# The deformable "snake" stage: four slope items handed to TensorE unsummed, and the offset convolution on shifted copies in four column tiles

## The reference, cut to what matters

```
off = tanh(group_norm(conv3x3(x, w_off, b_off)))      # the "offset convolution"; 9 of 18 channels are used
upper, lower = cumulative sums of off away from the centre channel 4
y = row + cumsum_k ; x = column + (k - 4)             # k = 0..8, nine sampling points
v_k = image sampled linearly between two rows at (y clipped, x clipped)
out = relu(group_norm(sum_k w_dsc[:, :, k] @ v_k + b_dsc))
x = x + out
```

## Time and profile before

| | us |
|---|---|
| median of 3 runs | 1713.78 (1711.48 to 1716.94) |
| the profiled execution | 1718.72 |
| its span from the first to the last instruction | 1715.8 |
| start of this stage (first instruction of its block) | 1362.06 |
| item 0 of pass 0 starts on DVE | 1402.80 |
| item 19 of pass 7 ends on DVE | 1699.2 |

### The profile page before, as it was taken

How to read it: one execution, slowest core, us unless ns; L and a number is a source line. 1 busy time by engine, 2 the same in 40 slices (tenths; PEclk the granted TensorE clock), 3 DMA queues, 4 the chain that set the end, 5 groups by cost and what they waited for, 6 DMA issues and landing times. The chain is left out here.

```text
span 1715.8 us, 35545 instructions
## 1 busy us (share of the span) xinstructions
PE 1445.7 (84%) x10772; PEld 643.9 (38%) x10772; DVE 1243.6 (72%) x4972; ACT 978.4 (57%) x1653; POOL 1083.2 (63%) x780
## 2 busy tenths in 40 slices
PE   3999999999999999999928999847777558786775
PEld 1333333333333333333306777536555322121211
DVE  4999999999998999999844445442222456767676
ACT  2588888888887888888823434310000024645454
POOL 3689999989998999999951223220000247867786
PEclk9999999999999999999968999979999879888877
DMA  6000000000000000000005555000000100000000
GB/s 146 8 2 9 4 9 4 10 5 2 9 4 10 5 2 11 2 2 2 2 17 111 111 111 110 0 19 0 0 0 0 44 0 1 1 1 13 1 13 25
DMA packets 16179, 35.48 MB, mean 21 GB/s; under 512 B 5636, under 2 KB 7272, under 8 KB 15996
## 3 DMA queue, kind: packets, MB, share of 16 engines
q1 hardware_dynamic: 14268, 31.96, 8.3%
q10 hardware_dynamic: 1728, 1.35, 0.3%
HBM read 9.47 MB, written 2.10 MB: 7 GB/s over the span
## 5 line engine op out<-in xcount | busy, mean ns | idle before, releaser
L440 POOL TENSOR_SCALAR l_onehot<-l_ib,c_iota 128x512 bf16<-128x512 f16 x256 | 399.9, 1563 | 60.7 <-ACT l_ib L387 60.7
L549 DVE FIND_INDEX8 l_idx<-l_top,l_scored 128x8 uint32<-128x256 f32 x1024 | 411.9, 416 | 0.0
L250 PE MATMUL ps<-l_ct_slot,l_res 32*128 32x512 f32 x2048 | 410.1, 612 | 0.0
L566 DVE CUSTOM_DVE_ANT_0 l_scored<-ps,l_gain 128x256 f32<-128x256 f32 x1024 | 375.8, 412 | 20.4 <-ACT l_gain L369 19.6
L369 ACT ACTIVATE l_gain<-ps 128x768 f32<-128x768 f32 (+1 forms) x384 | 283.8, 739 | 118.3 <-PE ps L250 117.6
L1603 POOL TENSOR_TENSOR l_isum<-l_term 128x512 f32<-128x512 f32 x160 | 204.9, 1309 | 89.1 <-DVE l_term L1701 50.3
L273 PE MATMUL ps<-l_onehot,l_cbp_slot 128*32 128x512 bf16 x3072 | 217.1, 390 | 7.0 <-POOL l_onehot L440 3.3
L244 PE MATMUL ps<-l_csq,l_row_slot 32*128 32x512 bf16 x1024 | 155.1, 396 | 20.3 <-DVE l_top L566 7.3
L250 PEld LDWEIGHTS ps<-l_ct_slot,l_res 32*128 32x128 f32 x2048 | 155.6, 194 | 11.5 <-issue 0.9
L1528 ACT ACTIVATE ps<-ps,l_minus 128x512 f32<-128x512 f32 x192 | 118.2, 662 | 72.6 <-DVE l_term L1707 56.4
L735 PE MATMUL ps<-l_wc,l_xi 100*128 100x192 f32 x768 | 133.4, 331 | 30.7 <-DMA l_xi<-l_xt 30.7
(11 more groups left out here) (158 smaller groups left out, 2048.9 us busy)
## 6 DMA issues: line engine op xcount, KB each, us to landing
l_xi<-l_xt SPq DMA_DIRECT2D x48, 384.0 KB, 7.1
X<-in_x SPq DMA_DIRECT2D x16, 128.0 KB, 7.9
out<-X SPq DMA_DIRECT2D x16, 128.0 KB, 2.2
l_ct<-in_codes_t SPq DMA_DIRECT2D x4, 448.0 KB, 13.5
l_ct_slot<-l_ct SPq DMA_DIRECT2D x7, 256.0 KB, 2.3
l_cbp_slot<-l_cbp SPq DMA_DIRECT2D x8, 96.0 KB, 1.9
l_wt<-in_l_w SPq DMA_DIRECT2D x1, 768.0 KB, 4.3
l_w_off<-in_l_w_off SPq DMA_DIRECT2D x1, 576.0 KB, 3.3
```

Of the source, the lines that this page charges most:

```text
L250: pe.matmul(ps[:, at + n - FIRST[k], :], res[rows, i, P * tt:P * (tt + 1)], ct_slot[rows, par, :], start=False, stop=True, skip_group_chec ...
L440: nc.gpsimd.tensor_scalar(onehot[:, i % 2, g, 0, :], ib16[:, i % 2, g, :], iota[:, 0:1], None, ALU.is_equal).then_inc(s_near, 1)
L549: nc.vector.max_index(idx8[:, i % 2, n, :], top[:, i % 2, n:n + 1].to_broadcast([P, 8]), scored[:, WIDE * (k % 3) + n - FIRST[k], :]).then ...
L566: nc.vector.tensor_tensor_reduce(out=scored[:, WIDE * (k % 3) + m, :], in0=ps[:, WIDE * (k % 2) + m, :PAIRED], in1=gain[:, WIDE * (k % 2) ...
```

## The change

- `DIRECT = 4`: the eight terms of items 0 to 3 go into a ring of four new buffers `slope_term` (`SLOPES = 4`) and PE takes them itself. The new `slope_terms(p, d)` is one group of four for one item (its two terms in the place of two items). POOL adds only items 4 to 19; `terms(p, i)` has 8 turns instead of 10. The wait on `s_partial` moves to `slope_terms(p, 0)`. DVE waits for `s_taken` before it writes a slope buffer again, so item 2 waits until PE has taken item 0.
- The offset convolution reads `xi`, in which SP lays three copies of each image shifted by 0, 1 and 2 columns side by side in 96 partitions (12 DMAs of 32 x 1154 fp32 for each set, 48 in all). One row ky of the 3 x 3 kernel is then four multiplications 96 x 32 x 512, one for each group, each in column tile g. `w_off` shrinks from 128 x 1152 to 96 x 96 fp32.
- PE's hand-written order is new: where the running sums, `own_rows`, `join`, the group averages and the pieces of the convolution stand. `copy_raw(1, j-1, 1)` and `moments(1, j-1, 1)` stand two items later. `down` and `bend` have two slots. The image differences on POOL come after item 4's addition, not item 3's.

```
+DIRECT = 4
+PAIRED_ITEMS = NI - DIRECT
+TURNS = PAIRED_ITEMS // 2
...
+            def columns(j):
+
+                sp.wait_ge(s_xz, START + j + 1)
+                if j:
+                    sp.wait_ge(s_conv, START + 2 * j)
+                flat = xz[:, j].rearrange("p y x -> p (y x)")
+                for g in range(G):
+                    for kx in range(3):
+                        sp.dma_start(xi[C * kx:C * kx + C, g, :SHIFTED],
+                                     flat[C * g:C * g + C, kx:kx + SHIFTED]).then_inc(s_xi, 16)
...
-            def offset_conv(j, h, taps):
...
+            def offset_conv(j, h, kys):
+
+                for ky in kys:
+                    if ky == 0 and h == 0:
+                        pe.wait_ge(s_xi, START + (j + 1) * (16 * 3 * G))
+                    for g in range(G):
+                        at = (ky + ROWS * h) * PADW
+                        rows = xi[:, g, at:at + ROWS * PADW].rearrange("p (y x) -> p y x", x=PADW)
+                        mm = pe.matmul(grid(ps[C * g:C * g + C, SIDE, :]), w_off[:, ky, :], rows[:, :, 0:W],
+                                       start=(ky == 0), stop=(ky == 2), skip_group_check=True)
...
+            def slope_terms(p, d):
+
+                pe.wait_ge(s_term, START + p * NT + 2 * d + 2)
+                if d == 0 and p:
+                    pe.wait_ge(s_partial, START + 2 * p)
+                at = 2 * (p * DIRECT + d)
+                operands = [(ITEMS[d][0], lambda rows, b=(at + e) % SLOPES: grid(slope_term[rows, b, :]))
+                            for e in range(2)]
+                accumulate(operands, d == 0, False).then_inc(s_taken, 1)
...
+                for d in range(DIRECT):
+                    slope_terms(p, d)
+                    if d == 0:
+                        running_sum(p, CUMS + 1)
...
+                for i in range(TURNS):
+                    for c in {0: (4, 5), 2: (6,), 3: (7,)}.get(i, ()):
+                        running_sum(p, c)
...
                     terms(p, i)
...
-                        if i == 1 and j:
-                            pe.wait_ge(s_raw[1], START + 2 * j - 1)
-                            join(p - 1)
-                        if i < 3:
-                            own_rows(p, i)
...
+                        if i == 0:
+                            if j:
+                                pe.wait_ge(s_raw[1], START + 2 * j - 1)
+                                join(p - 1)
+                            own_rows(p, 0)
+                        if i == 1:
+                            own_rows(p, 1)
+                            own_rows(p, 2)
...
-                for n in range(NI):
+                for n in range(DIRECT, NI):
...
-                    if j + 1 < J and n == 3:
+                    if j + 1 < J and n == DIRECT:
                         slope(j + 1) if h == 0 else bow(j + 1)
...
+                        if n < DIRECT:
+                            use = 2 * (p * DIRECT + n) + e
+                            if use >= SLOPES:
+                                dve.wait_ge(s_taken, START + (use - SLOPES) // 2 + 1)
+                            dst = grid(slope_term[:, use % SLOPES, :])
```

More of the change, by code:

```diff
@@ L1230, in block_l3 @@
         xe = t("xe", [P, J, EPITCH, EPITCH])
-        down = t("down", [P, J, EPITCH - 1, EPITCH])
-        bend = t("bend", [P, J, EPITCH - 2, EPITCH])
-        w_off = t("w_off", [P, 9, P])
+        down = t("down", [P, 2, EPITCH - 1, EPITCH])
+        bend = t("bend", [P, 2, EPITCH - 2, EPITCH])
+        w_off = t("w_off", [3 * C, 3, C])
         w_dsc = t("w_dsc", [P, SNAKE, P])
@@ L1260, in block_l3 @@
         s_xz = sem("xz")
+        s_xi = sem("xi")
         s_xe = sem("xe")
@@ L1298, in _ @@
             sp.wait_ge(s_in, START + 16 * LOADS3)
+            def columns(j):
[7 more added lines that the diff above has]
+                                     flat[C * g:C * g + C, kx:kx + SHIFTED]).then_inc(s_xi, 16)
+            for j in range(J):
+                columns(j)
             for j in range(J):
@@ L1315, in group_average @@
                           start=True, stop=True).then_inc(s_gavg[norm], 1)
-            def offset_conv(j, h, taps):
-                for n in taps:
-                    ky, kx = divmod(n, 3)
-                    mm = pe.matmul(grid(ps[:, SIDE, :]), w_off[:, n, :],
-                                   xz[:, j, ky + ROWS * h:ky + ROWS * (h + 1), kx:kx + W],
-                                   start=(n == 0), stop=(n == 8))
-                if taps[-1] == 8:
+            def offset_conv(j, h, kys):
[7 more added lines that the diff above has]
+                                       start=(ky == 0), stop=(ky == 2), skip_group_check=True)
+                if kys[-1] == 2:
                     mm.then_inc(s_conv, 1)
@@ L1430, in _ @@
                             group_average(1, j - 1, 0)
-                        if j and i == 6:
+                        if j and i == 4:
                             group_average(1, j - 1, 1)
-                        if i == 7:
+                        if i in (3, 4):
+                            own_rows(p, i)
+                        if i == 5:
                             if j:
@@ L1438, in _ @@
                             join(p - 1)
-                    if i == NI // 2 - 1 and p + 1 < PASSES:
-                        for c in range(CUMS, 2 * CUMS):
-                            if h == 0 and j + 1 < J:
-                                offset_conv(j + 1, 1, range(c + 4, c + 5))
-                            running_sum(p + 1, c)
-                        if h == 0 and j + 1 < J:
-                            offset_conv(j + 1, 1, range(8, 9))
             pe.wait_ge(s_raw[1], START + PASSES - 1)
@@ L1586, in bow @@
                 pool.wait_ge(s_down, START + j + 1)
-                nc.gpsimd.tensor_tensor(bend[:, j], down[:, j, 1:, :], down[:, j, :-1, :],
+                nc.gpsimd.tensor_tensor(bend[:, j % 2], down[:, j % 2, 1:, :], down[:, j % 2, :-1, :],
                                         ALU.subtract).then_inc(s_bend, 1)
```

91 lines of the change are left out of this document (47 added, 44 removed).

## The result

The changed kernel takes **1731.31 us** (median of 5 runs, 1729.27 to 1733.45), the one before 1713.78 (5 runs beside it): ratio **1.0097**, 95% interval 1.0075 to 1.0119. It is 17.5 us slower where 1.5 was predicted, and lies just above the range (1700 to 1730). The profiled execution took 1732.97 us, with a span of 1731.1; before it was 1718.72.

The account below looks back on a forecast made before the run. No engine fills a pass; waits on PE's ordered list, above all DVE's for running sums, bound the kernel. Passes -0.5, slow clock at transitions 2, start 0: +1.5 on 1713.78 gives 1715 us, range 1700 to 1730.

Parts of the forecast that it names:

- three waits: New waits: item 2 for slope buffers (2.5 us), item 8 behind POOL's image difference (2.5), item 10 behind six PE groups.
- F: Within a pass, when item 5's addition ends: S + 15.3 in even passes, S + 14.1 to 14.8 in odd ones.
- the convolution: Offset convolution on PE: column-tile groups at 1.0 to 1.09 us, 10.8 us less PE work in passes 0, 2 and 4.
- tiles in series: Rival: four fp32 column tiles run one after the other, 3.4 us a group; +45, 1760 us; chance 0.03.
- bare loads: Rival: weight loads of the new groups not hidden, 0.77 us a group; +12, 1727 us; chance 0.04.
- the start: Ahead of pass 0: shorter loads, then 12 copies and the first set's convolution; difference -1 to +1.5, taken as 0.
- +2: Extra outside the pass sum: PE on the slow clock in one of three transitions, 2.7 us, counted as 2.
- S: Start of item 0 in a pass, from which the forecast counts its times; item 2 was put at S + 4.9.
- a short wait 3 (2.7 and 1.2 us): Passes 6 and 7, without image difference: item 10 waits 2.7 and 1.2 us; passes forecast at 31.5 and 29.6.
- the sum of pass 6: Forecast length of pass 6: 31.5 us against 32.1 before.
- wait 3: Item 10 waits for a running sum behind six PE groups, starting at F + 8.1; 7 us lost by mid even pass.
- the slow clock held through wait 3: Rival: the six groups ahead of item 10 all run slow, 10.6 instead of 7.7 us; +14, 1728 us; chance 0.20.

Follow-up runs that it names:

- the move against it: Changed kernel with one edit each: running sum 6 taken earlier, image difference at the start of POOL's pass, or eight slope buffers with running sum 3 first: 1714.39, 1711.12, 1704.49 us.
- the convolution alone: Kernel before with only the new column-tile convolution, slope products still through POOL and the old order of running sums: 1698.33 us, ratio 0.9873.
- the fillers in the middle: Changed kernel plus zero-weight matmul groups on PE ahead of each pass's first `terms` (five in passes 0 to 5, two in 6 and 7): 1715.51 us.
- fillers at the transition: Changed kernel plus four zero-weight matmul groups on PE at the end of passes 1, 3 and 5: 1726.16 us, ratio 1.0070.
- both sets of fillers: Changed kernel plus zero-weight groups both at the end of passes 1, 3 and 5 and ahead of each pass's first `terms`: 1714.01 us, ratio 0.9982.

## Where the prediction held and where it failed

**Right: that the freed time would not be gained time**, and which three waits would stand against it. Each is in the trace at its place, and the move against it gave back 19, 24 or 28 us. In pass 2 item 10 was named to the tenth, and that was luck: F came 0.6 us earlier than worked out (item 2 waited 1.73 us, not 2.5), and the way from F to item 10 was 0.6 longer (8.7, not 8.1, because three groups and not two were slow). Passes 1, 2, 3 and 5 came within 0.35 us.

**Right: the convolution.** Between 0.93 and 1.07 us a group, as taken. The rivals of tiles in series and of bare loads are out: the convolution alone made the kernel 1.3% faster. The loads of the new groups are hidden in this trace. The rule that the prediction took from the Trainium skill ("TensorE: Matmul & The Clock Gate", Part 3, The mechanism), that a weight load overlaps only matmuls of other row groups, would have put 4.6 us a pass where none are. The same section also says that PE pulls a load ahead when it goes to a background weight buffer; the hidden loads fit that sentence. What the new convolution gives back was a little less than worked out: 21.5 us in passes 0, 2 and 4, or 7.2 each, against the 4.12 + 3.65 + 1.4 = 9.2 of pass 2.

**Right: the start** (0 predicted, -1.25 measured ahead of pass 0). One reading in it was wrong: of the 18 first streams some six were slow, not ten, since the 18 took 10.63 us against 7.99 at full clock, 0.43 more for each slow one. The tail, taken as unchanged, was 1.3 longer, two of its groups running at half clock.

**Wrong: "+2" for the slow clock at transitions.** The step said "in one of three transitions it may be on the slow clock, where `terms` and two slope groups cost 0.9 each: 2.7 us". The price was right, 2.7 us (S + 6.9 against S + 4.2), but it was counted once and fell on two passes, 4 and 6. In pass 0 the slow clock met the convolution (16 matmuls in 3.11 us, where they took 1.93 with the fillers in the middle), and behind it ACT's copy and ramps kept DVE waiting 2.60 us instead of 0.94. Pass 0 was 2.9 too long, pass 4 2.65. Pass 0 varies, though: up to its end the kernel with fillers at the transition has the same program in it and took 37.24 us instead of 38.69.

The kernel before had a slow stretch at the end of pass 3 too, but there nobody waited for PE: its granted clock was 0.50 from 1550 to 1559.4, DVE's waits in that time were for ACT's ramps, and pass 4 started at 1559.5. In the changed kernel the clock was 0.50 from 1561 to 1571, and pass 4 started at 1562.6. At the transition into pass 6 the trace of the kernel before could have warned (columns as in the earlier trace rows):

```profile
1642.00:1652.00 10.00, 7.87 (x35) 1.34 (x27) 6.31 (x11) 4.22 (x7) 7.98 (x7) 0.50 0.21 55
```

Pass 6 starts at 1640.0 there, and 2 us into it the clock is at half speed for 10 us.

**Wrong: "a short wait 3 (2.7 and 1.2 us)" in passes 6 and 7.** It measured 4.36 and 2.52. Six groups stand ahead of running sum 6 there as elsewhere; even at full clock the fillers' kernel waits 2.78 and 1.42. The 2.7 and 1.2 us are thus about the price at full clock: the slow clock was priced into wait 3 of the passes with an image difference and left out where there is none.

**Wrong in the sum of pass 6.** The prediction gives 31.5 without its terms. If it was built as that of pass 7 is (25.6 of DVE's work, plus 2.5, plus the short wait 3), it has no room for the waits that pass 6 had before. Counted as waits it comes out: in the changed kernel DVE waits 4.39 + 0.78 (items 2 and 3), 4.36 (item 10) and 2.15 (item 0 of pass 7) = 11.7; before it was 1.27 + 2.37 + 1.72 and 1.00 = 6.4. The difference, 5.3, is the 5.2 that the pass grew by.

Together these steps hold what the passes missed, 10.9 us (308.8 measured against 297.9 with the extra 2): some 6.3 for the slow clock in passes 0, 4 and 6, 3.0 for wait 3 in passes 6 and 7, and 1.5 for the rest of pass 6. The median is 16.0 us above the forecast; what is left of that lies in the start of the stage and the tail, and in the differences between executions, and was not followed up.

Of the rivals, the slow clock held through wait 3 (1728) came nearest in time. Its mechanism was only half of it: in pass 2 three of six groups were slow, as the forecast had it, and the extra time lay elsewhere. How much of the total is clock can't be split off cleanly. The fillers in the middle show that in the changed kernel it costs at least the 14.5 us of the passes that they gave back; how much the kernel before lost to it in the same places was not run, so this is no share of the 12.4 us that the passes grew by.

## What to carry to other kernels

When a change bundles a part that frees an engine with one that adds waits, price each by itself and look at the places where only one of them applies: here the last two passes, which had nothing to gain. A queue in program order pays for every group put ahead of a result that another engine waits for; moving three such lines (a running sum, an image difference, a buffer count) was worth 52 us, more than either half of the change, though less than the three gains added up. Count the slow clock at every place where the thinned-out engine became critical, not once in three, and in passes that have no new gap of their own as well. Build every forecast of a stretch on its measured length, or list the old waits that a sum from bare work leaves out.

## What the runs showed of the hardware

- Four fp32 column tiles of 96 rows by 32 columns run beside each other: three groups of 512 columns in 2.78 us, with their weight loads hidden (the 24 loads take 0.11 to 0.14 us each on their own).
- Useless matmuls can make a kernel faster: with five groups of them ahead of the first terms of a pass (two in the last passes), the changed kernel fell from a ratio of 1.0097 to 0.9982.
- The granted clock does not follow the idling next to it alone. With both sets of fillers it was 1.2 GHz at the transition into pass 4, behind a pass granted 0.98. At the end of pass 3 the kernel before was granted 0.50 in one stretch of about 10 us that ended as pass 4 began; the changed kernel, with a similar list of PE work, in two, of about 3 us and, across the transition, of 10 us.
- Twelve copies of 144.2 KB within on-chip memory, issued from 1372.62 on, had all landed when PE began at 1382.88: 1.77 MB in 10.3 us, 173 GB/s or more.
